# The order of TensorE's work inside a step of the attention bodies

## The reference

```
qk = jnp.einsum('nqhd,nkhd->nhqk', q, k)
qk = jnp.where(mask == 0, jnp.asarray(1e-20, qk.dtype), qk)
attn = jax.nn.softmax(qk / jnp.asarray(np.sqrt(E), qk.dtype), axis=3)
out = jnp.einsum('nhqk,nkhd->nqhd', attn, v).reshape(n, q_len, H * D)
return out @ Wo.T + bo
```

## Time and profile before

| what | value |
|---|---|
| median of 3 runs | 5331.87 us (5326.46 to 5332.09) |
| the profiled execution, its own time | 5328.68 us |
| its span | 5327.0 us |
| granted clock, mean | 0.872 |
| TensorE matmuls busy | 4330.9 us (81%) |
| VectorE busy | 3321.3 us (62%) |
| ScalarE busy | 2128.3 us (40%) |
| first and last scores by key, layer 0 | 208.5 to 805.1 us |
| the same, layer 2 | 3610.6 to 4007.0 us |
| the same, layer 3 | 4594.3 to 4993.6 us |

### The profile page before, as it was taken

The page is one execution under the profiler, slowest core; times in us unless marked ns, Lnnn a source line. Parts: engine busy times, 40 slices in busy tenths (PEclk is TensorE's granted clock), DMA queues, the critical chain, the costliest instruction groups (busy, mean ns, idle before and its releaser), DMA issues. The chain is left out here.

```text
span 5327.0 us, 86304 instructions
## 1 busy us (share of the span) xinstructions
PE 4330.9 (81%) x31716; PEld 3113.2 (58%) x31716; DVE 3321.3 (62%) x7267; ACT 2128.3 (40%) x3668; POOL 809.1 (15%) x478
## 2 busy tenths in 40 slices
PE   5699995999766999795478888559997897699888
PEld 4344444777655777674367777544554666355566
DVE  6566653444475666544855544458885887688576
ACT  2255552222112333342033333226775673477510
POOL 4423310000051000000012222310001233100000
PEclk8799997999877999897579999778997888799888
DMA  6222211000021000010034433441210004222000
GB/s 205 71 75 67 75 33 43 1 0 0 23 87 33 16 16 16 24 42 29 0 118 105 109 100 98 123 154 57 65 52 17 0 0 152 73 66 67 30 16 16
DMA packets 171769, 302.70 MB, mean 57 GB/s; under 512 B 22556, under 2 KB 90830, under 8 KB 171480
## 3 DMA queue, kind: packets, MB, share of 16 engines
q1 hardware_dynamic: 158824, 280.59, 16.7%
q0 software_dynamic: 12672, 18.42, 1.8%
HBM read 216.60 MB, written 80.77 MB: 56 GB/s over the span
## 5 line engine op out<-in xcount | busy, mean ns | idle before, releaser
L1552 ACT ACTIVATE a_pT<-a_psS 128x512 f32<-128x512 f32 x1536 | 836.0, 597 | 398.0 <-PE a_psS L1438 392.7
L1624 DVE TENSOR_REDUCE a_mx<-a_psA 128x1 f32<-128x512 f32 x1024 | 656.5, 685 | 82.3 <-PE a_psA L1416 82.2
L1416 PE MATMUL a_psA<-a_ks,a_qs 48*128 48x512 f32 (+1 forms) x1536 | 403.9, 521 | 156.9 <-PEq L46 93.7
L1453 PE MATMUL a_psZ<-a_pT,a_V 128*17 128x128 f32 x12288 | 488.1, 278 | 0.0
L1620 DVE CUSTOM_DVE_ANT_0 a_scored<-a_psA,a_hide_q 128x512 bf16<-128x512 f32 x512 | 332.7, 688 | 190.6 <-PE a_psA L1416 189.6
L1453 PEld LDWEIGHTS a_psZ<-a_pT,a_V 128*17 128x17 f32 x12288 | 272.6, 97 | 271.7 <-issue 158.5
L1416 PEld LDWEIGHTS a_psA<-a_ks,a_qs 48*128 48x128 f32 (+1 forms) x1536 | 151.0, 191 | 403.9 <-issue 174.6
L1438 PE MATMUL a_psS<-a_qs,a_ks 50*128 50x512 f32 (+1 forms) x1536 | 317.9, 407 | 2.8 <-ACT a_pT L1552 0.8
L2894 DVE SCALAR_TENSOR_TENSOR ex_h<-ex_psU,ex_ub,ex_sg 128x512 f32<-128x512 f32 x129 | 96.9, 751 | 318.3 <-PE ex_psU L159 311.3
L740 DVE TENSOR_TENSOR m_h_l<-m_h,m_h_h 128x512 fp32r<-128x512 f32 x64 | 44.3, 693 | 267.6 <-ACT m_h_h L684 265.5
L157 PE MATMUL m_psH<-m_xe_h,m_w_h 128*128 128x512 f32 x512 | 210.7, 411 | 0.0
(11 more groups left out here) (554 smaller groups left out, 11198.4 us busy)
## 6 DMA issues: line engine op xcount, KB each, us to landing
a_k_parts<-a_p_kp SPq DMA_DIRECT2D x96, 256.0 KB
a_q_parts<-a_p_qp SPq DMA_DIRECT2D x96, 256.0 KB
a_qs<-a_q_parts SPq DMA_DIRECT2D x192, 128.0 KB
a_ks<-a_k_parts SPq DMA_DIRECT2D x192, 128.0 KB
X<-in_L_ffn_gw SPq DMA_DIRECT2D x36, 512.0 KB
X<-in_L_ffn_up_w SPq DMA_DIRECT2D x36, 512.0 KB, 3.6
X<-in_L_ffn_down_w SPq DMA_DIRECT2D x36, 512.0 KB, 3.8
a_p_cT<-in_ctxT SPq DMA_DIRECT2D x24, 512.0 KB, 7.4
```

The costliest lines, as they stand in the source:

```text
L1416: nc.tensor.matmul(psA[:, unit(a, par) % 3], qs[r, g % ring, p % 2, q * P:(q + 1) * P], ks[r, g % ring, p % 2], start=True, stop=True).the ...
L1453: last = nc.tensor.matmul(psZ[q * VP:q * VP + VW, g % 2, j * P:(j + 1) * P], V[:, b, kt, g % NG * GH + j, :], pT[:, p % 2, par, kt, q * P: ...
L1552: nc.scalar.activation(pT[:, p % 2, par, kt, :], psS[:, unit(t, par) % 3], ACT.Exp).then_inc(exp_done, 1)
L1624: nc.vector.tensor_reduce(mx[:, p // 2 % 2, par, p % 2, q:q + 1], psA[:, unit(a, par) % 3], AX_X, ALU.max).then_inc(a_used, 1)
```

## The change

Only TensorE's program changes, in the loop over steps. In each step the scores by query come first, then the values, then the masks where there are any, then the scores by key, and last, as before, what `found` puts there.

```diff
                 for t in steps:
+                    if t + LEAD < QUARTERS:
+                        maxima_scores(t + LEAD)
+                    if TB <= t < QUARTERS + TB:
+                        values(t)
                     if hidden is not None and 0 <= t < QUARTERS:
                         hide_keys(t)
-                    if t + LEAD < QUARTERS:
-                        maxima_scores(t + LEAD)
                     if 0 <= t < QUARTERS:
                         exp_scores(t)
-                    if TB <= t < QUARTERS + TB:
-                        values(t)
```

## The result

The changed kernel takes 5431.99 us (median of 4 runs, 5416.9 to 5440.3) against 5331.98 (4 runs, 5326.5 to 5340.6): 1.0183 times the time of before, 95% interval 1.0155 to 1.0211. It is slower, as forecast, but by 100 us and not by 29, and it lies outside the stated range. The profiled execution took 5427.21 us.

A forecast was written before the change was run, and what follows sets the result against it. Plain steps: layers 2 and 3 bound by scores and DVE's maximum, layer 0 by masks, scores and ACT's exponential. +27.5 us ("heads") and 0 (layer 0) gave 5359.4; with a little for first and last groups 5361 us, range 5338 to 5390.

The forecast's parts named there:

- The step that failed: Layer 0 steps with extra work: already PE-bound, "heads" step 2.26 us before and 2.25 after, "sums", "turn", "out" likewise nothing.
- The prediction's own sign of being wrong: Wrong if "heads" finds the copy ready, layers 2 and 3 plain steps leave 1.28, or layer 0 moves over 20 us.
- "heads", layers 2 and 3: PE reaches "heads" before ACT's copy is done and waits, 0.43 us a group, 64 times, +27.5 us.
- Layer 0, plain steps: Masks' wait for ACT goes; a plain step falls from 1.95 to 1.66 us, 66 steps, -19 us.
- rival C: Layer 0: values to masks cost 0.56, not 0.46, over about 175 steps, +17 us, kernel 5378; chance 16%.
- Layer 0, behind "heads": Scores by query wait longer for DVE; the step grows from 2.00 to 2.43 us, 25 steps, +11 us.
- Layer 0, the loads: Loads issued behind ACT's copy land later, +1.0 us in each of seven groups, +7 us.
- A: Layer 0: the masks' wait for ACT comes back in full, at most 47.5 us, kernel 5312; chance 6%.
- B: No change: layer 0's plain gain of 19 us stays, not taken back by DVE or loads, kernel 5340; chance 11%.
- D: Granted clock falls after about 1.5 us of PE idle in layer 0, eight places, +24 us, kernel 5385; chance 7%.

The follow-up runs named there:

- experiment 5: Against the kernel before, only the masks moved, between scores by query and scores by key, with values last: 5378.5 us, 1.0088.
- experiment 1: Changed kernel with "heads" one step later (8g+13 instead of 8g+12): 5413.9 us, 1.0156.
- experiment 2: Changed kernel with values first, then scores by query, masks and scores by key: 5391.5 us, 1.0118.
- experiment 3: Changed kernel with values first and also "heads" one step later: 5435.3 us, 1.0201.
- experiment 6: Changed kernel with the psZ work (max, heads, turn, out, sums) put between values and masks: 5469.5 us, 1.0264.
- experiment 4: Changed kernel reordered to masks, scores by key, scores by query, values: 5304.2 us, 0.9956 of the kernel before.

## Why the prediction was wrong

**The step that failed** is the price of TensorE's own work in the new order: "A step with extra work was PE-bound already: 2.26 with "heads" before, 1.66 + 0.59 = 2.25 after; "sums", "turn" and "out" likewise nothing", and in layers 2 and 3 no term at all for "max", "turn" and "out", nor for the "heads" step beyond its wait. It added up distances between neighbours as if they belonged to the instruction. The 0.34 and 0.32 of the earlier trace rows hold for a pair next to the other pair, whose stream hides its weight load. Apart, as in experiment 5, each is 0.43 to 0.44. Measured from scores by key to scores by key, in layers 2 and 3 a "turn" step went from 1.81 to 2.01, "out" from 2.29 to 2.48, "max" from 1.55 to 1.68, and "heads" from 1.81 to 2.51; without its wait, in experiment 1, it is 2.01, so 0.50 goes with the wait and 0.20 is left. The bodies have 14, 25, 29 and 29 of them between the first and last scores by key, which makes some 17 us for each body beside the waits. In layer 0 the steps with psZ work lost 0.26 to 0.32 each, 125 of them, some 38 us: 0.20 of each for the pairs, and 0.10 because masks, whose load had run unseen behind psZ work, stand behind values now. Experiments 2, 3 and 5 show the pairs' part, 6 in its "out" steps; the part of the masks is read from the rows. The weight-load rows of the kernel before already held both, though no row that I showed did. The prediction's own sign of being wrong, layer 0 moving by more than 20 us, came true.

**"heads", layers 2 and 3: right.** Forecast 0.43 a group, measured 0.46 to 0.47 of idle (14.6 us over 31 in layer 2's body), and 0.50 by the length of the step. The mechanism was as worked out; that the size came so near is in part luck, since two terms were off and nearly cancel. PE's idle time begins 1.79 behind the scores by key of the step before (3852.49 to 3854.28) and not 1.61, as the pairs are apart. ACT's copy starts 1.51 behind them and not 1.39, since they last 0.50, and "heads" starts 0.15 behind the copy's end (3854.59) and not 0.05, at 2.25 instead of 2.03.

**Layer 0, plain steps: right in kind, wrong in size.** From 1.95 to 1.77, not 1.66. The term is values to masks: 0.57 and not the 0.46 derived from "heads" to masks; it is the other bound, rival C's. The pair of rows that it was derived from had a hidden load in it (601.47, above), as the rest of the failed step had. The rule of the Trainium skill (TensorE: Matmul & The Clock Gate, Weight-path perf modes) that bf16 weights load faster agrees with the load's own 98 ns, but behind values it bought nothing here.

**Layer 0, behind "heads": right.** Forecast 2.43, measured 2.42 to 2.43. Experiment 5, where scores by query follow "heads" too, has 2.44; experiments 2 and 4, where values or masks follow it, have 1.96 and 1.76: the loss needs scores by query right behind "heads", so that PE gets back to them before DVE is through.

**Layer 0, the loads: wrong, small.** Forecast +7. Idle time put down to them in layer 0's scores by query is 5.3 us for the matmuls and 8.5 for their weight loads, against 7.1 and 12.6 before. A likely reason, not tested, is that the steps in between had grown by themselves, so that the landing came no later relative to them.

**The rivals.** A (the wait comes back in full) and B did not come; C was right in its mechanism, but its 17 us are a quarter of the 71 by which the forecast for the kernel missed. D did not come in the changed kernel: the bodies' granted clock is 0.98 to 0.99. It came in experiments 1 and 3, behind 3.33 and 2.94 us of idle.

**Sum of what was measured**, for the profiled pair, step by step between the first and last scores by key: in layers 2 and 3 the waits of "heads" make 29 us (58 x 0.50) and the pairs apart 34; in layer 0 the steps with psZ work make 38, those behind "heads" 11, and the plain ones -14. Together that is 98, against 99.9 measured. In the forecast's terms, it lacked 34 for the pairs and 2 for the longer waits in layers 2 and 3 and, in layer 0, 25 for the pairs (125 x 0.20) and 17 for the masks (C's term), less the 7 for the loads that didn't come.

## What to carry to other kernels

A matmul's cost on TensorE belongs to it and its neighbours: before reordering, read from the weight loads' own timeline which loads run under another matmul, and keep those neighbours together. When work is moved behind something that another engine evacuates in order, work out how far behind that engine's last input the dependent instruction now arrives; here 1.79 us against the 2.25 at which it could start. If a wait can be taken away by an order that keeps both (here masks, scores by key, scores by query, values), the gain is real: a ratio of 0.9956 here.

## What the runs showed of the hardware

Two pairs of matmuls of 48 and 50 rows that use the same two row groups cost 0.66 us back to back and 0.87 with anything else between. The second pair's 0.19 us weight load (3803.05) runs during the first pair's stream (to 3803.41), so it doesn't wait for the row groups that it loads to be idle. Full-height bf16 masks load their weights in the same way behind full-height fp32 "heads" (601.47). Behind the values, which fill 17 columns each, neither load runs ahead: the loader is idle for 0.21 us and the load starts with its own matmuls (3853.77, 601.29), and behind the masks the pair's load does the same after 0.42 us (601.83). In these rows a load runs ahead behind work that is tiled as its own; whether it is the tiling that must agree, or something else that such neighbours share, was not tried.

Behind waits of 2.94 us the granted clock fell to 0.50, the 1.2 GHz level, once for 30 us in which TensorE was busy for 29.3 of 30, and once with 1.00 again 5 us later; behind one of 3.33 us it was at 0.50 up to 561.00. So the length of the wait doesn't fix that of the dip. Waits of 0.46 us in every group of 13 us left it at 0.98 to 0.99.
